# Expert outputs stored tile by tile in list order and added to each block by indexed reads; seven dense blocks instead of nine

## What is computed

```
f  = layernorm(x)
x1 = x + f @ W_self + (segment_sum(f[src], dst) / max(degree, 1)) @ W_neigh + b
xn = layernorm(layernorm(x1)) * gamma + beta
logits = xn @ Wr + br;  top 2 of 8 experts, weights = softmax of the two logits
out = x1 + sum over the 2 chosen experts e of  weight_e * (gelu(xn @ W1[e] + b1[e]) @ W2[e] + b2[e])
```

## Time and profile before

| | |
|---|---|
| three runs | 1312.43, 1315.35, 1317.46 us; median 1315.35 |
| the profiled execution | 1316.61 us |
| its span on the core | 1314.6 us, mean granted TensorE clock 0.968 of full |
| PE busy | 1155.8 us, 88% of the span |
| POOL busy | 960.6 us, 73% |
| DVE busy | 879.9 us, 67% |
| ACT busy | 424.9 us, 32% |
| bytes moved | 276.16 MB, mean 210 GB/s |

### The profile page before, as it was taken

One profiled execution on the slowest core, in us unless ns is written; L12 is line 12 of the kernel. 1 busy time (PEld: TensorE's weight loads), 2 busy tenths in 40 slices (PEclk: granted clock), 3 DMA queues, 4 the chain that ended last, 5 costly groups with the idle time before them and its releaser, 6 DMA issues.

```text
span 1314.6 us, 22817 instructions
## 1 busy us (share of the span) xinstructions
PE 1155.8 (88%) x6764; PEld 1030.2 (78%) x6765; DVE 879.9 (67%) x2835; ACT 424.9 (32%) x795; POOL 960.6 (73%) x1039
## 2 busy tenths in 40 slices
PE   0269999999988989999998999999888897999978
PEld 0248888888977879898897988988777795888867
DVE  6946666677677576877666677786587775664536
ACT  5503333323324333343342333343233331311121
POOL 6577777777767777777777777777777777777752
PEclk9978999999989999999998999999899998999989
DMA  9887765656655666666666756667557677677657
GB/s 334 263 259 226 221 194 178 189 168 197 206 165 171 200 193 209 189 210 205 197 221 185 214 183 191 204 212 245 178 168 228 224 235 237 224 236 219 222 165 233
DMA packets 154938, 276.16 MB, mean 210 GB/s; under 512 B 26464, under 2 KB 76896, under 8 KB 154688
## 3 DMA queue, kind: packets, MB, share of 16 engines
q1 hardware_dynamic: 103792, 142.94, 33.8%
q0 software_dynamic: 45456, 124.27, 30.9%
q10 hardware_dynamic: 5568, 7.47, 1.8%
HBM read 236.72 MB, written 37.86 MB: 209 GB/s over the span
## 4 chain that ended last, share of the span: by engine, by line
PE 73%; DVE 16%; issue 5%; DMA 2%; ACT 2%; POOL 1%; DVEq 1%; SPq 0%; ACTq 0%; POOLq 0%
PE bank L927 22%; PE bank L1003 19%; PE bank L1029 11%; PE bank L1037 9%; PE bank L915 3%; PE bank L956 3%; PE bank L958 3%; DVE heap L1417 2%; DVE agg L1274 2%; ACT heap L766 1%; DMA heap<-in_x 1%; PE bank L973 1%; DVE onehot L1220 1%; POOL ring L660 1%; PE bank L1053 1%
## 5 line engine op out<-in xcount | busy, mean ns | idle before, releaser
L660 POOL DMA_INDIRECT ring<-feature_table,src_sb x768 | 748.6, 975 | 252.5 <-issue 220.6
L927 PE MATMUL bank<-ring,onehot 128*128 128x257 f32 x1568 | 394.8, 396 | 84.8 <-DVE onehot L1220 52.6
L927 PEld LDWEIGHTS bank<-ring,onehot 128*128 128x128 f32 x1568 | 307.7, 199 | 140.4 <-issue 82.6
L1417 DVE TENSOR_TENSOR heap<-bank,b_sb 128x512 f32<-128x512 f32 x157 | 108.4, 691 | 224.7 <-PE bank L1003 83.5
L828 ACT ACTIVATE heap<-heap 128x512 f32<-128x512 f32 x157 | 98.9, 630 | 429.8 <-DVE heap L1417 429.8
L1029 PE MATMUL bank<-heap 128*128 x680 | 170.5, 395 | 18.4 <-DVE inside L1426 6.2
L1003 PE MATMUL bank<-row_t,heap 128*128 128x128 f32 x1360 | 166.8, 276 | 1.8 <-DVE heap L1417 1.8
L1003 PEld LDWEIGHTS bank<-row_t,heap 128*128 128x128 f32 x1360 | 161.1, 193 | 3.7 <-issue 2.6
L1029 PEld LDWEIGHTS bank<-heap 128*128 128x128 f32 x680 | 127.8, 196 | 36.9 <-issue 21.1
L1037 PE MATMUL bank<-heap 128*128 128x256 f32 x576 | 142.5, 391 | 15.8 <-DVE agg L1452 8.8
L1003 PE MATMUL bank<-dst_i,heap 128*128 128x128 f32 x1152 | 141.6, 276 | 0.6 <-DVE heap L1417 0.6
(11 more groups left out here) (179 smaller groups left out, 1241.7 us busy)
## 6 DMA issues: line engine op xcount, KB each, us to landing
heap<-in_w SPq DMA_DIRECT2D x314, 256.0 KB
ring<-feature_table,src_sb POOLq DMA_INDIRECT x768
row<-expert_rows SPq DMA_DIRECT2D x85, 129.0 KB, 4.1
xf<-in_x SPq DMA_DIRECT2D x49, 128.0 KB
ff<-feature_table SPq DMA_DIRECT2D x49, 128.0 KB
feature_table<-heap SPq DMA_DIRECT2D x6, 896.0 KB, 5.7
heap<-in_w SPq DMA_DIRECT2D x4, 1024.0 KB, 5.7
heap<-in_w ACTq DMA_DIRECT2D x16, 256.0 KB
```

Source lines behind the costliest of these rows:

```text
L660: pool.indirect_dma_start(ring[:, q * GT + i, 0:D], None, x if t < RAW else table, bass.IndirectOffsetOnAxis(src_sb[:, k:k + 1], 0)).then_ ...
L927: last = pe.matmul(bank[t % 2][:, 0:D + 1], onehot[:, q, i, :], ring[:, q * GT + i, :], start=(i == 0), stop=(i == GT - 1))
L1417: dve.tensor_tensor(hid[S.slot(u, 2)], hidden_b[:, :].rearrange("p (k t) -> p k t", k=HK), b1_sb[:, bass.ds(e, 1), :].rearrange("p o k -> ...
```

## The change

**1. Results are stored whole, in list order.** A tile's 128 weighted rows are stored by SP as one plain DMA to `expert_out`, at the row where the tile starts in its list (`store_rows`, a new step `store` two slots after `weigh`). The 85 indirect puts on POOL are gone, and so is the column that carried the place (R = D + 1). `store_rows` waits until the tile is weighted and until all tiles but the one before it are stored; it reads the start row from `list_i` into a register.

**2. A block's rows are fetched by index and added in place.** `slots` keeps the two list rows of every node in `slots_of`. Merging a block is now two indirect DMAs on POOL (`take_rows`), each of which reads 128 rows of `expert_out` and adds them to x1 in `agg` on the way (`compute_op=ALU.add`). The second waits until the first has landed. In the slot loop the first stands in slot `at`, the second in `at + 2`. After the loop the other blocks follow, the second fetch two blocks behind the first. SP stores `agg` directly. `load_pair` and all additions of L686 and L1409 are gone.

**3. The lists are shorter and prefilled.** A list has room for `SHARE` = 2176 rows instead of 6400 in the planned pass, and `share_claim` checks the counts. Since a planned tile can hold empty rows and a fetch must never meet foreign bytes, SP fills the first 8 x 2176 rows of `expert_out` with zeros, 68 DMAs of 256 KB, two per slot in slots 10 to 43.

**4. Seven dense blocks, not nine.** 15, 21 and 33 become routed and 18 becomes dense. That removes 16 dense units and adds two routed blocks (four scatters) and four list tiles (89). There are now 41 merged blocks, 23 of them in the slot loop.

```diff
-CONSTS = 20
+CONSTS = 16
 EMPTY = 18
+SHARE = 17 * P
-DENSE_BLOCKS = (0, 3, 6, 9, 15, 21, 27, 33, 47)
+DENSE_BLOCKS = (0, 3, 6, 9, 18, 27, 47)
-MERGE_CLAIMS = ((28, 8), (32, 16), (36, 20), (40, 24), (44, 28))
-MERGE_BUFFERS = 10
-MERGE_BEHIND = 6
+MERGE_CLAIMS = ((28, 12), (32, 16), (36, 20), (40, 24), (44, 28))
+MERGE_SEMS = 4
+MERGE_BEHIND = 2
...
-              "weigh": (5, 2), "add": (9, 5)}
+              "weigh": (5, 2), "store": (7, 4), "add": (9, 5)}
...
-    R = D + 2
+    R = D + 1
-    CAP = NP + P
+    CAP = 3 * SHARE
+    FILLS = NE * SHARE // (2 * P)
...
# SP
             def store_merged(i):
-                k = merge_buffer[i]
-                sp.wait_ge(merged, i + 1)
-                io, _ = merge_io[k]
-                sp.dma_start(nodes(out, NB - 1 - merges[i][0]), merge_b[k][:, 0:D]).then_inc(io, 16)
+                sp.wait_ge(taken[i % MERGE_SEMS], 32 * (i // MERGE_SEMS + 1))
+                sp.dma_start(nodes(out, NB - 1 - merges[i][0]), x1_of(main, merges[i][0])).then_inc(d_out, 16)
...
             def load_rows(S, j):
-                tiles_put(hold, S, S.freed(j, XR))
+                hold(S.y_set, S.freed(j, XR))
...
+            def store_rows(S, j):
+                if S.planned:
+                    tiles_put(hold, S, max(j - 1, 0))
...
+                hold(S.y_set, j + 1)
+                if S.planned and j == 0:
+                    sp.wait_ge(trash_out, 16 * (FILLS + EMPTY + 1))
+                at, = load_values(mybir.EngineType.SP, list_i[0:1, bass.ds(j, 1), 1], NE * CAP + (EMPTY - 1) * P, **unchecked)
+                sp.dma_start(expert_out[bass.ds(at, P), :], y_out[S.slot(j, XY)][:, :]).then_inc(S.y_put[S.slot(j, 2)], 16)
...
+                for i in range(FILLS):
+                    if t == 2 * HK + 2 + i // 2:
+                        two = expert_out[2 * P * i:2 * P * (i + 1), :].rearrange("(p c) d -> p c d", c=2)
+                        sp.dma_start(two, empty_row[:, 0:D].unsqueeze(1).broadcast_to([P, 2, D])).then_inc(trash_out, 16)
+                for j in tiles_in(t, "store"):
+                    store_rows(main, j)
-                for i in merges_in(t, -1):
+                for i in merges_in(t, -4):
                     store_merged(i)
-                for i in merges_in(t, 2):
-                    load_pair(i)
...
# POOL
-            def put_rows(S, j):
...
-                pool.indirect_dma_start(node_rows, bass.IndirectOffsetOnAxis(row[S.slot(j, XR)][:, D + 1:R].bitcast(I32), 0),
-                                        y_out[S.slot(j, XY)][:, :], None).then_inc(S.y_put[S.slot(j, 2)], 16)
+            def take_rows(i, c):
+                n, of_list, at = merges[i]
+                pool.wait_ge(taken[i % MERGE_SEMS], 32 * (i // MERGE_SEMS) + 16 * c)
+                if c == 0:
+                    tiles_put(hold, main, lists[of_list][1])
+                pool.indirect_dma_start(x1_of(main, n), None, expert_out[0:NE * SHARE, :],
+                                        bass.IndirectOffsetOnAxis(slots_at(main, n)[:, c:c + 1], 0),
+                                        compute_op=ALU.add).then_inc(taken[i % MERGE_SEMS], 16)
...
                 for n in routed_in(t, "scatter"):
                     scatter_rows(main, n)
-                for j in tiles_in(t, "add"):
-                    put_rows(main, j)
-            for i in range(STAGE_MERGES, len(merges)):
-                add_pair(i)
+                for i in merges_in(t, -2):
+                    take_rows(i, 1)
+                for i in merges_in(t):
+                    take_rows(i, 0)
+            for i in range(STAGE_MERGES, len(merges) + MERGE_BEHIND):
+                if i < len(merges):
+                    take_rows(i, 0)
+                if i >= STAGE_MERGES + MERGE_BEHIND:
+                    take_rows(i - MERGE_BEHIND, 1)
```

More of the change, by code:

```diff
@@ L150, in build @@
     UNITS = EARLY + NJ
-    merge_buffer = [i % 2 if at is not None else i % MERGE_BUFFERS for i, (n, c, at) in enumerate(merges)]
-    merge_use = [merge_buffer[:i].count(merge_buffer[i]) for i in range(len(merges))]
     STAGE_MERGES = len([at for n, c, at in merges if at is not None])
@@ L244, in build @@
         rows = [sb(f"rows{s}", [P, 2, R]) for s in range(XP)]
-        slot_i = [sb(f"slot_i{s}", [P, 2], I32) for s in range(XP)]
         sums_t = [sb(f"sums_t{s}", [P, 2 * DK, P]) for s in range(2)]
@@ L286, in build @@
         assert 2 * D + DK * P <= NT
-        pair = sb("pair", [P, 2 * D])
-        ring_flat = ring[:, :, :].rearrange("p a b -> p (a b)")
-        merge_b = [dst_i[:, DK * P:DK * P + 2 * D].bitcast(F32), pair[:, :]]
-        merge_b += [ring_flat[:, k * 2 * D:(k + 1) * 2 * D] for k in range(MERGE_BUFFERS - 2)]
+        again_b = dst_i[:, DK * P:DK * P + 2 * D].bitcast(F32)
         snap = sb("snap", [1, len(MERGE_CLAIMS), NE])
-        late = sb("late", [1, len(MERGE_CLAIMS) + 1])
+        late = sb("late", [1, len(MERGE_CLAIMS) + 2])
         row = [sb(f"row{s}", [P, R]) for s in range(XR)]
@@ L394, in build @@
         halved, merged = sem("halved"), sem("merged")
-        merge_io = [(s, 16) for s in x_in] + [(sem(f"merge_io{k}"), 0) for k in range(MERGE_BUFFERS - len(x_in))]
+        taken = [sem(f"taken{k}") for k in range(MERGE_SEMS)]
         LAST = NB - 1
@@ L507, in close_lists @@
                     ends = load_values(mybir.EngineType.SP, end_i[0:1, e0:e0 + 4], NE * CAP - P, **unchecked)
-                    for e, end in enumerate(ends):
-                        sp.dma_start(rows_tab[bass.ds(end, P), :], empty_row[:, e % 2, :]).then_inc(S.ends_out, 16)
+                    for end in ends:
+                        sp.dma_start(rows_tab[bass.ds(end, P), :], empty_row[:, :]).then_inc(S.ends_out, 16)
                 sp.wait_ge(S.ends_out, 16 * NE)
@@ L592, in _ @@
                 sp.wait_ge(edges_done, 1)
+                for i in range(EMPTY):
+                    sp.dma_start(rows_tab[NE * CAP + i * P:NE * CAP + (i + 1) * P, :], empty_row[:, :]).then_inc(trash_out, 16)
                 load_nodes(again, 0, 0)
@@ L602, in _ @@
                     load_w1_of(again, j)
+                    store_rows(again, j)
                 def merge_again(n):
-                    io, base = merge_io[0]
-                    sp.dma_start(merge_b[0], node_rows[bass.ds(n * (2 * P), 2 * P), :].rearrange("(p c) d -> p (c d)", c=2)).then_inc(io, 16)
-                    hold(merged, n + (len(merges) + 1))
-                    sp.dma_start(nodes(out, n), merge_b[0][:, 0:D]).then_inc(io, 16)
-                    hold(io, n * 32 + (base + 32 * (merge_buffer.count(0) + 1)))
-                sp.wait_ge(again.y_put[0], 16 * NJ_ALL)
+                    hold(merged, n + 1)
+                    sp.dma_start(nodes(out, n), again_b[:, 0:D]).then_inc(edges_done, 16)
+                    hold(edges_done, n * 16 + 17)
                 merge_again(0)
@@ L723, in _, with take_again @@
                     scatter_rows(again, n)
-                put_rows(again, 0)
-                with pool.Fori(1, NJ_ALL) as j:
-                    put_rows(again, j)
                 pool.wait_ge(again.y_put[0], 16 * NJ_ALL)
+                def take_again(n):
+                    hold(edges_done, n * 16 + 1)
+                    pool.tensor_copy(slot_2[:, :], slots_of[:, bass.ds(NB - 1 - n, 1), :].rearrange("p o c -> p (o c)")).then_inc(m_idx, 1)
+                    hold(m_idx, n + (NT + 1))
+                    for c in range(2):
+                        pool.indirect_dma_start(again_b[:, c * D:(c + 1) * D], None, expert_out,
+                                                bass.IndirectOffsetOnAxis(slot_2[:, c:c + 1], 0)).then_inc(m_gathered, 16)
+                take_again(0)
+                with pool.Fori(1, NB) as n:
+                    take_again(n)
         @block.scalar
@@ L1510, in _ @@
                             merge_claim([n for n, m in MERGE_CLAIMS].index(n))
+                if t == block_at["list"][NB - 3] + 4:
+                    share_claim()
                 for n in routed_in(t, "slots"):
@@ L1540, in _ @@
                     degrees(main, n, NB - 1 - n)
-                for i in merges_in(t):
-                    add_pair(i)
-                    add_x1(i)
-            for i in range(min(STAGE_MERGES + 3 * NE, len(merges)), len(merges)):
-                add_x1(i)
             n_miss = dve.value_load(missed_i[0:1, 0:1], min_val=0, max_val=2 * NT * P)
```

113 lines of the change are left out of this document (42 added, 71 removed).

## The result

| | before | after |
|---|---|---|
| median of 4 runs, us | 1315.7 (1312.4 to 1317.5) | 1345.1 (1344.5 to 1346.2) |
| span of the profiled execution, us | 1314.6 | 1343.9 |
| granted TensorE clock, slots 140 to 180 | 0.96 | 0.92 |
| last group of the slot loop begins, us | 1262.2 | 1261.9 |
| from there to the end of the span, us | 52.4 | 82.0 |

The ratio of the runs is 1.0227 (95% interval 1.0205 to 1.0249). The change is slower by 29.4 us. The forecast was 1285 us, so it missed by 60 us and had the sign wrong.

The account below looks back on a forecast made before the run. POOL was taken as full, PE nearly so, with POOL leading after slot 140. The last group would come 40 us earlier and the end give back 8.6, so span 1283.2 and execution 1285 us, range 1272 to 1318.

Parts of the forecast that it names:

- The price of a fetch: POOL, each adding fetch: taken as 1.33 us, like the put it replaces, between bounds of 1.28 and 1.98 us.
- three descriptors: Rival: POOL writes three entries per row instead of two, price 1.80 us, 1319 us in all; chance 0.14 with prices near it.
- the upper bound of 1.98: Fetch price if it cost a gather plus the addition POOL does itself for a pair; would give 1333 us.
- Slots 4 to 60: PE leads, so no gain; the new zero fills could cost between 0 and 53 us, taken as 2 us.
- Slots 60 to 140: POOL leads: 42.5 us less work and 5 us less waiting give 474 us, against 442 us of PE work.
- Slots 140 to 180: POOL leads: 32 puts go and 40 fetches come, +10.6 us, so 285 instead of 274 us; PE is covered.
- Slots 180 to 195: POOL loses nine puts and gets three fetches (-8 us), but the gain stops at the 5 us PE waits.
- The end: After the last tile's store, 36 fetches on POOL take 47.9 us and replace PE's dense chain, giving back 8.6 us.
- The chain of landings: Rival at the end: fetches land only after 5.2 us and pace the 18 pairs, 15 us more, 1300 us; chance 0.09.
- The fills: Rival in slots 10 to 43: zero fills make loads or gathers late; a third of 53 us gives 1303; chance 0.10.
- The slow second pass: Rival: the planned lists do not hold and a second pass makes the time several times as long; given no chance.
- The dear fetch: Rival, 43 loop and 36 end fetches: gain used up at 1.75 us, 1333 us at 1.98; chance 0.11 (over 1318).

Follow-up runs that it names:

- fetch_plain: The changed kernel with every fetch a plain gather that overwrites the rows, the addition to x1 left out: 1293.9 us, the kernel before 1312.7 on the same chip.
- even: The changed kernel with dense units spread more evenly over slots 60 to 140, by one number of the planner's spacing: 1341.1 us.
- fetch_plain_end: The changed kernel with only the 36 fetches behind the loop made plain gathers, without the addition to x1; those in the loop still add: 1327.5 us.
- dve_add: The changed kernel with both rows of a block fetched by plain gathers and added to x1 by VectorE, on a slower chip: ratio 0.9884 to the kernel before.
- dve_add_b: The changed kernel with plain gathers and VectorE adding to x1, on a chip of usual speed: 1292.2 us against 1315.1 before, ratio 0.9833.
- early_end_b: The changed kernel with plain gathers, VectorE adding, even dense spacing and some merges moved right behind POOL's last gather, on a slower chip: 1590.2 us against 1625.9, ratio 0.9757.

## Why the prediction was wrong

**The price of a fetch was mis-sized; the mechanism, a full POOL that pays for it in the loop and at the end, was right.** "I take 1.33, the put that it replaces" is the step that failed. Measured is 1.86. The prediction named the price at which the gain is used up, 1.75, and 1.86 is over it. Of its two rivals with a dearer fetch, "three descriptors" (1.80) is nearest in price, the upper bound of 1.98 in outcome. The reason given for 1.33 ("an instruction that only writes descriptors; the adding lies in the DMA engines") does not hold, as `fetch_plain` shows: with source, destination and indices unchanged, the addition alone makes POOL's instruction longer by 0.60 us (0.946 to 1.544). The Trainium skill has the rule in "Collectives: The Full Stack", section "The bandwidth ceiling: the fold count and why AG ≠ RS ≠ AR", that an adding transfer needs two read descriptors per chunk; it says so of the reduce step of a collective, whose descriptors the host writes. Taken over to POOL, as the prediction's rival did, it would give an estimate of 1.5 times the busy time, and the trace has 1.63 times. That POOL writes a third descriptor per row is not shown by any run.

Point by point, by the prediction's own steps. Its times for the groups follow from its sum; the span was to be 1283.2.

| step | forecast | measured | missed by |
|---|---|---|---|
| group of slot 140 begins | 854.7 | 871.8 | 17.1 |
| slots 140 to 180 | 285 | 303.4 | 18.4 |
| slots 180 to 195 | 82.5 | 86.7 | 4.2 |
| last group to the end | 61.0 | 82.0 | 21.0 |
| sum | 1283.2 | 1343.9 | 60.7 |

*Slots 4 to 60.* Right: the fills are covered. Slot 60's group began 1 us earlier than before, not the 2 later that were allowed, a difference that single executions show as well.

*Slots 60 to 140.* The work was right: PE 447 us busy where 442 were forecast, and POOL, by its 371 instructions at 0.99 us and 0.30 behind each, 478 us. The waits were wrong. The prediction took 5 us off for them ("lose their reason where PE gets ahead"); of those in rows 3, which run to slot 196, 3.5 us for PE and 2.9 for DVE were in these slots. POOL's waits for PE rose instead, to 15.3 us, and POOL took 491.8 us, from 370.2 to 862.0, where 474 were forecast. The error was to hold two sums over 80 slots against each other. The dense units lie unevenly in them, 9 and 10 in some tens of slots and 3 to 6 in others. In the dense tens PE is busy nearly all the time and POOL waits for it; in the sparse ones POOL leads. `even` shows a part of it: with the same work spread more evenly the waits are 8.9 us and slot 140 comes 6 us earlier. Whether a still more even plan would take away the rest was not tried.

*Slots 140 to 180.* POOL leads, as forecast. 40 fetches at 0.53 us more are 21 us, and POOL took 304.8 us (862.0 to 1166.8) instead of 285.

*Slots 180 to 195.* 1.6 us are the three fetches, and nothing of a dearer fetch was absorbed here, though the prediction's sum for it had 3 us. The rest is where slot 180's group fell: `fetch_plain_end`, which is the same up to here, had 307.6 and 83.4 us where the change had 303.4 and 86.7, 391.0 against 390.1 together. From slot 140 to the last group 367.5 us were forecast, and 43 fetches at 0.53 us are 22.8 of the 22.6 missed.

*The end.* The forecast had the right chain, the landing of the last store (3.4 us allowed, 3.2 measured) and then the fetches. 36 times 0.53 us are 19 of the 21 us missed; most of the rest is POOL's wait for landings, 3.3 us, which takes the place of a few pauses of 0.30.

The price alone is 43 us of the 60.7 (82 fetches times 0.53). Some 15 us more were lost before slot 140, most of them in POOL's waits for PE: its instructions alone come to 478 us there, and it took 491.8. `fetch_plain` bears this out: with plain fetches at 1.25 us and everything else as forecast the span would have been 1277 (1283.2 less 79 times 0.08), and it is 1292. The 15 us between them are the second error.

*The other rivals.* The chain of landings did not come, though a fetch takes 4.0 us to land: POOL waited 3.3 us for them in all. The fills were covered. The slow second pass did not run.

*The chances.* The range (1272 to 1318) did not hold the time. The dear fetch and its neighbour had 0.25 together, and a slower kernel 0.15. Yet no row held the price of a fetch below 1.98 us, the bound that the prediction took from an addition done on POOL, and 82 instructions pay it. The break-even of 1.75 lies two thirds of the way from 1.28 to 1.98: with no reason to favour one price over another, a third would have been the chance of no gain. And the price alone would not have told the time: by the prediction's own formula 1.86 us give 79 x 0.53 - 3 = 39 us more, 1324 us. The 1345 measured needed the second error too, and the sum had no rival for it.

*Two readings.* What POOL waits for in rows 3 is 11.4 us (5.3 for PE and 6.1 for DVE), not under 10; nothing in the sum hangs on it.

## What to carry to other kernels

An indirect DMA that adds is not a free addition for the engine that issues it: here it cost POOL 1.86 us per 128 rows where a plain gather cost 1.25. On a full POOL, fetch plainly and let an engine with room add. Moving work off the leading engine paid (stores in list order by SyncE, with fewer dense blocks, gave 1.7% once the fetch was plain and VectorE added). The two go together: seven blocks without the stores cost 11 us, and the stores with nine blocks 19 us more than with seven.

Before taking one engine to lead through a long stretch, compare the two engines piece by piece, in pieces short against the lead that one can build up over the other. The ring is four groups deep here, and the load of ten slots was uneven enough to make POOL wait. Sums over the whole stretch hide this.

## What the runs showed of the hardware that was not expected

**Packets.** The page's rows of the software queue, first of the changed kernel, then of `fetch_plain`. They move the same bytes with a different number of packets.

```profile
DMA packets 185675, 289.70 MB, mean 216 GB/s; under 512 B 28048, under 2 KB 118288, under 8 KB 185424
...
q0 software_dynamic: 53376, 124.36, 34.4%
```

```profile
DMA packets 177803, 289.70 MB, mean 224 GB/s; under 512 B 28048, under 2 KB 107792, under 8 KB 177552
...
q0 software_dynamic: 45504, 124.36, 32.7%
```

The difference is 7872, which is 96 for each of the 82 fetches. Under 2 KB there are 10496 more, 128 for each. The simplest reading is that an adding fetch of 128 rows goes in 128 packets of a row each (1 KB), and a plain one in 32 packets of over 2 KB. That fits with the longer landing (4.0 us against 3.2). Whether it is also why POOL needs 0.60 us more no run tells.

**The clock.** In slots 140 to 180 nearly the same matmuls kept PE busy 248.0 us at a granted clock of 0.92 in the changed kernel and 240.4 us at 0.95 in `fetch_plain`. PE waited more in the changed kernel (55 of 303 us against 39 of 280). Whether that lowered the clock no run isolates. POOL leads there (slot 180's group comes 8.4 us behind its first gather), so the 8 us more of PE are not on the path.

**Slower chips.** On three chips every kernel took about 25% longer. POOL's gathers were as short as ever (0.973 us in `dve_add`, 0.974 in `dve_add_b`). The granted clock was lower, 0.89 against 0.96 in these two, and PE busy 1219.2 against 1114.6 us, which is 105 of the 336 us between them. DVE's longest wait is put down to something that the profile does not name ("remote"), on a line that at the usual speed waits for PE (L1430 in the one kernel is L1428 in the other). The rows are from `early_end_b`, then from `dve_add_b` on a usual chip.

```profile
DVE heap L1430 <- remote: 258.5, 53, 16.4
```

```profile
DVE heap L1428 <- PE bank L1011: 81.9, 58, 7.3
```

The mean transfer rate of `dve_add` was 178 GB/s against 225 for the same kernel on a usual chip. What holds the transfers or PE up there stays open. A chip's speed can turn a sign: seven dense blocks in the kernel before were 0.8% slower on a usual chip and 1.4% faster on a slower one, from one execution of it on each.
